# Forward W transform folded over the two halves of a row, in 64x32 tiles, with VectorE forming the sums and the differences

## What is computed

```python
# layer 0, with the real number Re - Im per frequency
f = fft2(x, axes=(1, 2), norm='ortho'); Xh = f.real - f.imag
o1 = relu(einsum('bhwni,nio->bhwno', Xk, w1[0]) + b1[0])
o2 = einsum('bhwni,nio->bhwno', o1, w2[0]) + b2[0]
x  = ifft2(softshrink(o2, 0.01), s=(H, W)).real + x
# layer 1, complex, on the result
xf = rfft2(x, axes=(1, 2), norm='ortho')
o1r = relu(xr @ w1[0] - xi @ w1[1] + b1[0]);  o1i = relu(xi @ w1[0] + xr @ w1[1] + b1[1])
o2r = softshrink(o1r @ w2[0] - o1i @ w2[1] + b2[0]);  o2i likewise
y  = irfft2(o2r + 1j * o2i, s=(H, W)) + x
```

## Time and profile before

| | us |
|---|---|
| median of three runs | 526.34 |
| lowest, highest | 525.83, 531.92 |
| the profiled execution | 527.67 |
| its span | 525.8 |

### The profile page before, as it was taken

One profiled execution on the slowest core, in us unless ns is written; L12 is line 12 of the kernel. 1 busy time (PEld: TensorE's weight loads), 2 busy tenths in 40 slices (PEclk: granted clock), 3 DMA queues, 4 the chain that ended last, 5 costly groups with the idle time before them and its releaser, 6 DMA issues.

```text
span 525.8 us, 14875 instructions
## 1 busy us (share of the span) xinstructions
PE 480.0 (91%) x6144; PEld 347.5 (66%) x6144; DVE 303.9 (58%) x674; ACT 208.8 (40%) x473; POOL 172.8 (33%) x194
## 2 busy tenths in 40 slices
PE   4549999999999999999999999999999999998772
PEld 1137777767777677767777676777777777876531
DVE  6413456456764577456764577456763677566642
ACT  0014544554354433554354433454345433433101
POOL 9703133113432134313442133312442123222124
PEclk9858999999999999999999999999999999999967
DMA  8859955476899588877889688886989565735397
GB/s 187 268 141 218 272 149 150 105 205 181 253 222 244 154 210 246 238 202 184 263 216 236 173 208 242 228 213 176 255 221 248 167 175 156 156 84 141 108 242 223
DMA packets 76720, 104.65 MB, mean 199 GB/s; under 512 B 7761, under 2 KB 63303, under 8 KB 76526
## 3 DMA queue, kind: packets, MB, share of 16 engines
q1 hardware_dynamic: 57622, 55.97, 39.8%
q0 software_dynamic: 10608, 40.45, 29.1%
q10 hardware_dynamic: 8424, 7.28, 5.5%
HBM read 52.23 MB, written 51.43 MB: 197 GB/s over the span
## 4 chain that ended last, share of the span: by engine, by line
PE 79%; DMA 6%; DVE 6%; POOL 3%; ACT 2%; issue 2%; SPq 1%; ACTq 0%; POOLq 0%; DVEq 0%
PE ps L605 13%; PE ps L669 13%; PE ps L694 12%; PE ps L656 11%; PE ps L572 10%; PE ps L618 9%; PE ps L681 5%; PE ps L634 4%; DMA scr_f<-fs 3%; PE ps L644 3%; DVE img L551 2%; DVE ns L525 2%; ACT p L442 1%; POOL img L386 1%; POOL xs L369 1%
## 5 line engine op out<-in xcount | busy, mean ns | idle before, releaser
L551 DVE TENSOR_TENSOR img<-ps,img 90x768 f32<-90x768 f32 x92 | 82.7, 900 | 23.0 <-PE ps L605 18.1
L369 POOL TENSOR_TENSOR xs<-xs,nt 128x360 f32<-128x360 f32 (+1 forms) x48 | 41.5, 865 | 149.3 <-DVE nt L503 121.7
L605 PE MATMUL ps<-jr,cst 64*128 64x384 f32 (+1 forms) x358 | 83.6, 535 | 7.2 <-DVE img L551 5.7
L572 PE MATMUL ps<-img,cst 128*64 128x384 f32 (+1 forms) x368 | 72.2, 506 | 12.4 <-DMA img<-x 7.6
L378 POOL DMA_DIRECT2D y<-img x42 | 34.6, 825 | 136.0 <-DVE img L551 135.6
L618 PEld LDWEIGHTS ps<-cst,bt 128*64 128x64 f32 x1472 | 63.2, 141 | 21.0 <-issue 13.9
L435 ACT ACTIVATE o<-ps,wt 97x180 f32<-97x180 f32 (+1 forms) x96 | 33.8, 405 | 107.2 <-PE ps L656 107.1
L618 PE MATMUL ps<-cst,bt 128*64 128x90 f32 x1472 | 69.0, 248 | 6.7 <-DMA bt<-scr_f 6.7
L525 DVE SCALAR_TENSOR_TENSOR ns<-p,ps 109x384 f32<-109x384 f32 x96 | 53.2, 554 | 37.9 <-ACT p L442 33.0
L669 PE MATMUL ps<-wt,o 128*64 128x96 f32 x1472 | 73.9, 250 | 0.5 <-DVE o L517 0.5
L669 PEld LDWEIGHTS ps<-wt,o 128*64 128x64 f32 x1472 | 64.9, 137 | 12.6 <-issue 12.6
(11 more groups left out here) (41 smaller groups left out, 411.5 us busy)
## 6 DMA issues: line engine op xcount, KB each, us to landing
y<-img POOLq DMA_DIRECT2D x35, 540.0 KB, 5.5
img<-x POOLq DMA_DIRECT2D x30, 540.0 KB, 8.5
scr_i<-et SPq DMA_DIRECT2D x48, 270.0 KB, 5.7
scr_f<-fs SPq DMA_DIRECT2D x176, 72.0 KB, 3.4
bt<-scr_f SPq DMA_DIRECT2D x40, 270.0 KB, 4.6
jr<-scr_i SPq DMA_DIRECT2D x48, 216.0 KB, 5.1
img<-x ACTq DMA_DIRECT2D x10, 540.0 KB, 7.4
y<-img SPq DMA_DIRECT2D x11, 270.0 KB, 3.8
```

Source lines behind the costliest of these rows:

```text
L369: nc.gpsimd.tensor_tensor(re, re, nt[s % 2][:, :, 0:kws(s), 0:H], ALU.subtract).then_inc(re_ok, 1)
L551: nc.vector.tensor_tensor(y, p, y, ALU.add).then_inc(i_add, 1)
L572: last = mm(ps[64 * r:64 * r + 64, P3 + g % 2, 0:(b - a) * HC], K["w_fwd"], img[t % IMGS][:, a:b, :].rearrange("p h c -> p (h c)"), start= ...
L605: last = mm(ps[:, B0 + r, 0:n], K["w_inv"][64 * r:64 * r + 64, :], set_rows(t, j)[64 * r:64 * r + 64, at, 0:n], start=True, stop=True)
```

## The change

A row of 90 values is folded at its middle: for even frequencies the cosines and sines of the two halves are equal, for odd ones they have opposite signs. So the even frequencies need only the sum of the halves and the odd ones only the difference, each with 45 values to add up.

- The image buffer is now [128, 23, 2, 192]: partitions 0 to 44 hold the image rows 0 to 22, partitions 64 to 108 the rows 23 to 44, and the axis of 2 is the half of the row. Every load and store of x and y is two DMAs of 45 partitions. A buffer moves in four chunks (of 16, 16, 8 and 5 rows of the image) and no longer six.
- A new item `uv` in the list: VectorE adds and subtracts the halves of four pairs of image rows into `uv` (two operations of 128x768). One pair of sums for the forward piece of the next step stands at a step's end, the other between E and C0.
- A forward piece (now line 618) covers eight image rows with eight matmuls in 64x32 tiles: two halves of the partitions, even and odd frequencies, two pairs of rows. It fills banks 6 and 7 and there are six per task, two in each of steps 1 to 3. ScalarE copies both banks, also in task 0. SyncE stores each piece with eight DMAs of 24 partitions.
- The scratch tensors have other layouts, and 96 slots take the place of 90 rows. E has 96 columns.
- The inverse has four 64x64 tiles per group. Groups now stand differently: two in step 3, three in step 4, four in step 5 and three in step 0, and the middle one stands between D1 and D0.
- Refills are items of their own: chunk 0 in step 5, chunk 1 in step 0, chunks 2 and 3 in step 1. There are four `jr` buffers and three `fs` buffers. VectorE and GpSimd clear whole image buffers at the start.

```diff
@@ schedule @@
+        first, last = inv[s][0:len(inv[s]) - 3] if len(inv[s]) > 3 else [], inv[s][max(len(inv[s]) - 3, 0):]
+        uv = [("uv",) + f[1:] for f in fwd[s]]
+        ahead = [("uv",) + f[1:] for f in fwd[s + 1]] if s + 1 < NSTEPS else []
...
-        order += inv[s][0:1]
+        order += first
         if s > 1:
             order.append(("e", s - 2))
-        order += inv[s][1:2]
+        order += uv[1:2]
+        order += last[0:1]
         if s < NSTEPS:
             order.append(("c0", s))
         if 0 < s <= NSTEPS:
             order.append(("d1", s - 1))
+        order += last[1:2]
         if s < NSTEPS:
             order.append(("d0", s))
+        if i == 5 and t > 0:
+            order.append(("refill", t - 1, 0))
+        if i == 0 and t > 1:
+            order.append(("refill", t - 2, 1))
...
-        order += fwd[s][0:2]
+        order += fwd[s][0:1]
...
-        order += fwd[s][2:4]
+        order += fwd[s][1:2]
...
-        order += inv[s][2:3]
+        order += last[2:3]
+        order += ahead[0:1]
@@ sync, forward stores @@
-                    for r in range(f_dmas(g)):
-                        a, b = h0 + 2 * r, min(h0 + 2 * r + 2, h1)
-                        sp.dma_start(scr_f[t][a:b].rearrange("h e k c -> (e k) h c"),
-                                     fs[k][64 * r:64 * r + 2 * KWP, 0:(b - a) * HC].rearrange("q (h c) -> q h c", c=HC)).then_inc(f_st[k], 16)
+                    for p in range(2):
+                        sp.wait_ge(f_cp, 2 * n + p + 1)
+                        for a in range(2):
+                            for o in range(2):
+                                sp.dma_start(scr_f[t][o * KWP // 2:(o + 1) * KWP // 2, :, p, g, a].rearrange("k e s c -> (k e) (s c)"),
+                                             fs[k][64 * a + 32 * o:64 * a + 32 * o + KWP, p, :]).then_inc(f_st[k], 16)
@@ gpsimd, y and refill @@
+                    pool.wait_ge(*added(t, g))
+                    for p in range(2):
+                        j0, j1 = jrange(*CHUNKS[c], p)
+                        pool.dma_start(rows_of(out[b], HR * p + j0, HR * p + j1, f), folded(k, p, j0, j1)).then_inc(y_st[k][c], 16)
@@ vector @@
+                if kind == "uv":
+                    t, g = what
+                    n, (j0, j1) = t * CH + g, jrange(g, g + 1)
+                    dve.wait_ge(*x_loaded(t, g))
+                    if n >= 2:
+                        dve.wait_ge(f_mm, n - 1)
+                    nc.vector.tensor_tensor(uv[n % 2][:, 0, 0:j1 - j0, :], img[t % IMGS][:, j0:j1, 0, :], img[t % IMGS][:, j0:j1, 1, :],
+                                            ALU.add).then_inc(u_ok, 1)
+                    nc.vector.tensor_tensor(uv[n % 2][:, 1, 0:j1 - j0, :], img[t % IMGS][:, j0:j1, 0, :], img[t % IMGS][:, j0:j1, 1, :],
+                                            ALU.subtract).then_inc(v_ok, 1)
@@ tensor, forward @@
-                    for r in range(f_dmas(g)):
-                        a, b = h0 + 2 * r, min(h0 + 2 * r + 2, h1)
-                        last = mm(ps[64 * r:64 * r + 64, P3 + g % 2, 0:(b - a) * HC], K["w_fwd"],
-                                  img[t % IMGS][:, a:b, :].rearrange("p h c -> p (h c)"), start=True, stop=True)
+                    for a in range(2):
+                        for o in range(2):
+                            for p in range(2):
+                                q, m = 64 * p, 64 * a + 32 * o
+                                last = mm(ps[m:m + 32, P3 + p, 0:2 * HC], w_fwd[q:q + 64, o, :],
+                                          uv[n % 2][q:q + 64, o, 2 * a:2 * a + 2, :].rearrange("w s c -> w (s c)"), start=True, stop=True)
```

More of the change, by code:

```diff
@@ L141, in schedule @@
             order += [("rows", t - 1, j) for j in range(JR)]
[L142 to L144 removed]
+        if i == 1 and t > 1:
+            order.append(("refill", t - 2, 2))
+        order += fwd[s][1:2]
+        if s < 3:
+            order.append(("x", 2 * s + 3))
         if 0 < s <= NSTEPS:
             order.append(("t", s - 1))
[L147 removed]
+        order += last[2:3]
+        order += ahead[0:1]
+        if i == 1 and t > 1:
+            order.append(("refill", t - 2, 3))
     order += held
[L149 removed]
+    order += [("rows", TASKS - 1, j) for j in range(CH)]
     order += [("inv", TASKS - 1, g) for g in range(GROUPS)]
@@ L265, in last_added @@
                 return i_pool, LAST_POOL.index(g) + 1
-            return i_add, (TASKS - 1) * GROUPS + len([m for m in range(g + 1) if m not in LAST_POOL])
+            return added(TASKS - 1, g)
         def block_no(t, n):
@@ L381, in _ @@
+                if kind == "refill" and what[0] + IMGS < TASKS:
+                    t, c = what
+                    k, (b, f) = t % IMGS, divmod(t + IMGS, HALVES)
+                    pool.wait_ge(y_st[k][c], 32 * (t // IMGS + 1))
+                    for p in range(2):
+                        j0, j1 = jrange(*CHUNKS[c], p)
+                        pool.dma_start(folded(k, p, j0, j1), rows_of(x[b], HR * p + j0, HR * p + j1, f)).then_inc(x_ld[k][c], 16)
                 if kind == "inv" and what[0] == TASKS - 1 and what[1] in LAST_POOL:
-                    t, g = what
@@ L383, in _ @@
-                    n, (h0, h1) = LAST_POOL.index(g), hrows(g)
+                    t, (g, r) = what[0], divmod(what[1], 2)
+                    n, (j0, j1) = LAST_POOL.index(what[1]), jrange(g, g + 1)
                     pool.wait_ge(i_act, n + 1)
-                    y = img[t % IMGS][0:W, h0:h1, :].rearrange("p (r s) c -> p r (s c)", r=2)
-                    nc.gpsimd.tensor_tensor(y, p1[0:W], y, ALU.add).then_inc(i_pool, 1)
-                if kind == "load" and what[0] % STEPS == 3 and what[0] // STEPS >= 2:
-                    refill(what[0] // STEPS - 2, NXC - 1)
+                    y = img[t % IMGS][0:ROWS, j0:j1, r, :]
```

326 lines of the change are left out of this document (167 added, 159 removed).

## The result

| | median us | runs |
|---|---|---|
| before | 526.9 | 525.8 to 531.9, 4 |
| changed | 600.0 | 597.6 to 602.0, 4 |

The ratio is 1.136, 95% interval 1.128 to 1.145. The profiled execution has a span of 600.2 us (before: 525.8), so 74.4 us have to be found. The direction of the forecast (550 us, 532 to 580) was right, its size was not.

The account below looks back on a forecast made before the run. TensorE bounds the tasks, so spared time counts unless a later wait eats it. From 527.7 us: start +11, task 0 -1, tasks +5.4, refills +8.5 make 551.6; the median runs 1.3 lower, so 550 us, range 532 to 580.

Parts of the forecast that it names:

- Refills, +8.5: Sums in tasks with a refill: landing takes 14.2 us against 12.5 available, 1.7 us wait in each of 5 tasks.
- just not late: Later tasks' load for A at step 5's end: 62 queued DMAs take 30 of some 38 us, 6 to land.
- The rival on the queues: Store queue makes the load 2 us late and refills wait 4 us each: 574 us; chance 0.12.
- Its price for sums that meet GpSimd's subtraction: VectorE sums and GpSimd subtraction exclude each other: up to 0.87 us per meeting, one per task's step 1, 5 us more.
- D0's wait in step 2: TensorE's D0 waits 1.03 us for C0's relu behind VectorE's sums, leaving step 2 at 9.35 against 9.71 us.
- 59.8 us for a task: Sum of the six steps without refill waits: 59.8 against 58.9 us, +0.9 per task, +5.4 over six tasks.
- The forward piece, 0.65: Eight 64x32 tiles on TensorE all run at once, so a forward piece takes 0.65 us instead of 1.30.
- Start, +11: 48 stores at 0.49 us each put the first A at 41.7 us; +8 if issued at 0.43, up to +14.
- VectorE hides the sums: Rival: sums cost 0.61 us or less, D0's wait vanishes and TensorE keeps the bound: 511 us; chance 0.06.
- most is hidden: Rival: start costs 5, refills are in time, steps even out: 530 us, within 2%; chance 0.12.
- four tiles for eight: Rival: only four tiles run at once, the forward piece stays at 1.30 us: 577 us; chance 0.08.
- The chance of slower: Probability given that the measurement shows the changed kernel slower: 0.80, against 0.14 within 2% and 0.06 faster.

Follow-up runs that it names:

- e3: Changed kernel with the refill loads left out, sums waiting only for the output store: 572.5 us (568 and 577).
- e2: Changed kernel with six one-group image chunks instead of four, refills issued earlier and the first task's image 1 loads earlier: 562.7 us, ratio 1.070.
- e16: e14 with output stores of groups summed early leaving in their step and chunk 4's refill issued at step 1's start: 536.7 us, ratio 1.024.
- e1: Changed kernel with the refills of chunks 0 and 1 issued half a step earlier, right behind C0: 619.0 us.
- e15: e14 with the eight tiles of the forward piece issued by row half: 563.7 us.
- e13: e2 with 64-row stores and GpSimd's image DMAs in its gap, refills ahead of stores, last output stores in their steps: 558.3 us.
- e14: e13 with one pair of sums per step moved behind C0's relu on VectorE: 561.0 us.

## Why the prediction was wrong, point by point

- **Refills, +8.5: the step that failed.** I set 14.2 us for a store and a refill at the mean rate against 12.5 us of room. The room was right: without its wait the sum would have started at 305.7, 12.4 us behind the store's issue (293.37). The mean rate was right too, 220 GB/s for 221. What was wrong is that the store and the refill had it to themselves: 3.79 MB were moved in place of 2.16, and the refill was there after 17.3 us. The row of landings has 14.7 us at its end where I had worked with a median of 8.5. The five waits were 3.4 to 5.3 us, 21.7 in sum, and not 1.7 each; and the clock behind them, which no term had, made 28 us of it, by step 1's times against e3's. e2 and e16 show that the wait goes at the same bytes or more, with smaller chunks and more lead together.
- **The same queues elsewhere: no term.** Task 0 (+8.6, I had -1: VectorE waits for image 1; gone in e2), the load of task 6 (4.6 us and its clock; I had it "just not late") and the rows of the last task (+6.9 from the last T to the end, I had 0 +- 2). The rival on the queues named loads 2 us late and refills 4 us; it was the right mechanism, but gave 574 us. Its price for sums that meet GpSimd's subtraction was not paid here, since they never met (L397 took 0.91 us at most); e1 shows the price where they do.
- **Steps: right in kind, short in size.** D0's wait in step 2 was 1.03 predicted, 0.97 measured; C1's in step 0 0.75 and 0.79; the sums 0.95 us each. That gave 59.8 us for a task and e3 shows 61.6 without refill waits. Half of the 1.8 is the forward piece's, next; 0.5 is step 5 (11.0 for 10.5); the rest lies in steps 2 and 3, and I have not found its cause.
- **The forward piece, 0.65: mis-sized.** The eight tiles do overlap, far below the 1.30 us of four at a time, but the piece has 0.80 us from its start to the next piece's:

```profile
326.31 0.54 PE L687 MATMUL ps<-o,wt 64*64 64x180 f32 x8 [0.97 <-DVE o L532]
326.78 0.88 PE L618 MATMUL ps<-uv,cst 64*32 64x384 f32 x16
327.58 1.46 PE L661 MATMUL ps<-cst,bt 128*64 128x90 f32 x32
```

  That is 0.15 x 6 = 0.9 us a task. I had argued it from C0's four tiles of 180 columns, and read them wrongly. C0 took 0.47 us and not the 0.63 of pairs, but full scaling would have been 0.67 x 180 / 384 = 0.31: the row already had 0.16 us over it, as much as the piece has over 0.65. Why tiles cost this much more no run shows; e15 rules out their order. Nothing in the rows had eight tiles.
- **Start, +11: too much.** The first A came at 38.15, not 41.7, 7.0 us later than before: the 48 stores took 20.5 us where I had 23.3, since the queue issues one every 0.43 us, my other bound.

```profile
12.88 20.52 SPq L327 DMA_DIRECT2D scr_f<-fs  x48
```
- **VectorE hides the sums, most is hidden, four tiles for eight**: these rivals were wrong. The sums cost 0.95 us and not 0.61, and the piece 0.80 and not 1.30. That 577 us, the number of the tiles, lies nearest to 600 is chance.
- The chance of slower was right; the range was too narrow. Its terms for the queues had nothing else on the engines, and none for the clock.

## What to carry to other kernels

Ask of each transfer how long before its use it can be issued, and count for its landing all bytes that will be on their way with it, those issued behind it too, or take the longest row; the median of the landings is too short. On an engine that computes and issues DMAs in order, a wait for a landing is a wait of everything behind it: smaller chunks, a step between store and refill, and both in the engine's gaps were worth most of 63 us here. Price a new wait of TensorE of some us with the slower clock behind it, and judge a reordering by its steps, not its total: e13 and e14 looked like failures with all but one step mended.

## What the runs showed that I had not expected

- Behind a gap of 5.3 us TensorE ran at half the granted clock for 3.6 us: D1 2.83 for 1.54 us.
- A DMA whose outer dimension is 2 lay on 2 of the 16 engines by the packet counts: 809 us for 556 with the same bytes as two DMAs of 64 rows each.
- Eight float32 tiles of 64x32 take 0.80 us for a piece that two of 128x64 do in 0.67 (half as many rows), whatever their order.
- Halves of 45 partitions instead of 90 cost 8 us at the same bytes. GpSimd's issue takes 0.66 us for 270 KB of 45 partitions, 0.77 for 540 KB of 45 and 0.82 for 540 KB of 90, so a half costs nearly as much to issue as the whole.
- VectorE's sum and GpSimd's subtraction, both with two operands in SBUF, slow each other when they meet: 1.63 us for 0.95 and 1.68 for 0.89 (e1).
